# First LayerNorm of a transformer block: statistics finished in four groups of four token tiles instead of one group of sixteen

## What is computed

```python
x = x + 0.5 * ffn(layernorm(x))        # routed "spline" FFN, 64 experts in 8 clusters, then a LayerNorm
x = x + attn(layernorm(x))             # causal, 16 query heads on 4 kv heads, LayerNorm, output projection
x = x + 0.5 * ffn(layernorm(x))        # the same FFN again

def layernorm(x, eps=1e-5):
    m = mean(x, axis=-1); v = var(x, axis=-1)
    return (x - m) / sqrt(v + eps)
```

## Time and profile before

| | us |
|---|---|
| median of 2 runs | 1165.7 (1164.79 to 1166.62) |
| the profiled execution | 1164.39 |
| span of its slowest core (core 1), first to last instruction | 1162.9 |
| spans of the 8 cores | 1151.6 to 1162.9 |
| busy on core 1: PE, ACT, DVE | 802.9, 511.3, 479.7 |

### The profile page before, as it was taken

How to read it: one execution, slowest core, us unless ns; L and a number is a source line. 1 busy time by engine, 2 the same in 40 slices (tenths; PEclk the granted TensorE clock), 3 DMA queues, 4 the chain that set the end, 5 groups by cost and what they waited for, 6 DMA issues and landing times.

```text
span 1162.9 us, 12643 instructions; the slowest of 8 cores (1151.6 to 1162.9 us)
## 1 busy us (share of the span) xinstructions
PE 802.9 (69%) x3804; PEld 322.3 (28%) x3804; DVE 479.7 (41%) x912; ACT 511.3 (44%) x497; POOL 13.7 (1%) x21
## 2 busy tenths in 40 slices
PE   3087561796999457587788788886069968766197
PEld 1053210334444113222222222222034325311032
DVE  1853815685000554533522241113225564580643
ACT  1061331006223455378888988997171006233100
POOL 0100000000000000000000000000000010000000
PEclk9988855555999566589999989998558996865555
DMA  6800000008000000000000000000500012000024
GB/s 153 187 2 0 1 0 0 1 1 109 1 1 1 1 0 1 1 1 1 1 1 1 1 1 1 1 1 1 73 1 1 1 12 21 1 1 0 0 117 173
DMA packets 23872, 25.24 MB, mean 22 GB/s; under 512 B 13178, under 2 KB 17531, under 8 KB 23810
## 3 DMA queue, kind: packets, MB, share of 16 engines
q0 software_dynamic: 12208, 7.09, 5.1%
q1 hardware_dynamic: 11602, 17.34, 4.6%
HBM read 23.13 MB, written 8.39 MB: 27 GB/s over the span
## 4 chain that ended last, share of the span: by engine, by line
PE 50%; ACT 19%; DVE 14%; issue 8%; DMA 6%; SPq 1%; DVEq 1%; ACTq 0%; POOL 0%; POOLq 0%
ACT sE L1395 11%; PE pQ L938 7%; PE pW L1324 5%; PE pO L1139 5%; PE pTR L361 5%; PE pS L1197 4%; PE pH L624 3%; ACT sHH L1395 3%; PE pD L855 3%; PE pD L844 3%; PE pD L849 3%; DMA sX<-x 3%; PE pM L698 3%; PE pS L677 2%; DMA sWV<-wv 2%
## 5 line engine op out<-in xcount | busy, mean ns | idle before, releaser
L1395 ACT ACTIVATE sE<-pS,sNB 128x1024 bf16<-128x1024 f32 (+1 forms) x320 | 296.8, 990 | 71.4 <-PE pS L1197 69.5
L1139 PE MATMUL pO<-sE,sVTM 128*65 128x512 bf16 (+3 forms) x640 | 194.6, 389 | 23.5 <-DVE sTMPA L1395 23.1
L1197 PE MATMUL pS<-sQT,sKT 64*128 64x512 bf16 (+3 forms) x640 | 124.7, 381 | 59.9 <-DVE sE L1395 32.9
L361 PE MATMUL pTR<-sIDB,sXFB 128*128 128x128 bf16 x512 | 73.5, 262 | 66.1 <-ACT sXFB L1395 65.8
L1395 DVE TENSOR_TENSOR sE<-sE,sTRI 128x256 bf16<-128x256 bf16 x128 | 37.1, 291 | 162.0 <-ACT sE L1395 161.3
L1197 PEld LDWEIGHTS pS<-sQT,sKT 64*128 64x128 bf16 x640 | 36.6, 94 | 178.9 <-issue 176.8
L361 PEld LDWEIGHTS pTR<-sIDB,sXFB 128*128 128x128 bf16 x512 | 53.0, 104 | 88.7 <-issue 70.2
L1395 ACT ACTIVATE sRS<-sSCR 128x16 f32<-128x16 f32 x6 | 1.4, 229 | 168.5 <-DVE sSCR L1395 168.5
L1139 PEld LDWEIGHTS pO<-sE,sVTM 128*65 128x65 bf16 x640 | 47.5, 115 | 96.0 <-issue 90.7
L1395 DVE BATCH_NORM_STATS2 sSTAT<-sX 128x6 f32<-128x512 f32 x96 | 60.3, 686 | 11.3 <-ACT sGB L1395 6.1
L1324 PE MATMUL pW<-sWO,sT 128*128 128x512 bf16 x256 | 62.4, 388 | 0.0
(11 more groups left out here) (176 smaller groups left out, 835.1 us busy)
## 6 DMA issues: line engine op xcount, KB each, us to landing
sX<-x SPq DMA_DIRECT2D x4, 2048.0 KB, 20.0
y<-sX SPq DMA_DIRECT2D x16, 512.0 KB, 2.6
sWQ<-wq POOLq DMA_DIRECT2D x1, 2048.0 KB, 17.5
sWO<-wo POOLq DMA_DIRECT2D x1, 2048.0 KB, 16.6
sW1C<-cw POOLq DMA_DIRECT2D x2, 512.0 KB, 11.1
sWK<-wk POOLq DMA_DIRECT2D x1, 512.0 KB, 22.0
sWV<-wv POOLq DMA_DIRECT2D x1, 512.0 KB, 24.5
sSGR<-sigsT SPq DMA_DIRECT2D x1, 256.0 KB, 19.0
```

The costliest lines, as they stand in the source:

```text
L361: tt.transpose(pTR[:, par, c, :], sXFB[:, par, 128 * c:128 * (c + 1)], sIDB[:]),
L1139: mi = t.matmul(pO[:, h, lv:512], sVTM[:, c, gg, :], sE[:, epar, h, lv:512], start=(c == 0), stop=(c == cmax - 1))
L1197: mi = t.matmul(pS[:, cpar, h, lv:512], sKT[o:o + 64, kchunk, 128 * c:128 * (c + 1)], sQT[o:o + 64, hp, q0:qe], start=True, stop=True, til ...
L1395: self._last = a(*args, **kw)
```

## The change

`emit_ln_stats` gets a branch `quarters`, used by the first LayerNorm alone. It takes the tiles in four groups: 8 `bn_stats`, then their 8 `bn_aggr`. The tail of a group (9 operations, the square root, 6 operations, now on 128 x 4 operands) is emitted behind the `bn_aggr` of the next group. `emit_ln_transpose` gets `aux_tiles`: the normalisation of tile t waits for the tail of its own group, not for one mark of all tiles. The number of `bn_stats` and `bn_aggr`, the arithmetic on each element, the transposes and the copies stay the same.

```diff
+    def emit_ln_stats(src_tiles, rs_out, tile_waits=None, quarters=False):
+        if quarters:
+            auxq = [None] * 4
+            agq = []
+            for q in range(4):
+                for t in range(4 * q, 4 * q + 4):
+                    ap = src_tiles(t)
+                    tw = tile_waits[t] if tile_waits else []
+                    P.st("v", lambda v, t=t, ap=ap:
+                         v.bn_stats(sSTAT[:, t, 0:6], ap[:, 0:512]), wait=tw)
+                    P.st("v", lambda v, t=t, ap=ap:
+                         v.bn_stats(sSTAT[:, t, 6:12], ap[:, 512:1024]))
+                sm = P.mark("v", "AUX")
+                for i, t in enumerate(range(4 * q, 4 * q + 4)):
+                    P.st("v", lambda v, t=t: v.bn_aggr(sMV4[:, t, 0:2], sSTAT[:, t, 0:6]),
+                         wait=[sm] if i == 0 else [])
+                    P.st("v", lambda v, t=t: v.bn_aggr(sMV4[:, t, 2:4], sSTAT[:, t, 6:12]))
+                agq.append(P.mark("v", "AUX"))
+                if q >= 1:
+                    auxq[q - 1] = emit_ln_stats_tail(rs_out, [agq[q - 1]],
+                                                     (4 * (q - 1), 4 * q))
+            auxq[3] = emit_ln_stats_tail(rs_out, [agq[3]], (12, 16))
+            return auxq
...
-    def emit_ln_stats_tail(rs_out, wait0):
+    def emit_ln_stats_tail(rs_out, wait0, ts=(0, NT)):
+        t0, t1 = ts
+        sMV4s = sMV4[:, t0:t1]
+        sSCRs = sSCR[:, t0:t1]
+        rs_out = rs_out[:, t0:t1]
...
-            w = list(aux_ready) if isinstance(aux_ready, list) else [aux_ready]
+            if aux_tiles is not None:
+                w = [aux_tiles[t]]
+            else:
+                w = list(aux_ready) if isinstance(aux_ready, list) else [aux_ready]
...
+        elif first:
+            tw = [[xld[t // 4]] for t in range(NT)]
+            aux = emit_ln_stats(lambda t: sX[:, t, :], sRS, tile_waits=tw, quarters=True)
...
-        lnv = emit_ln_transpose(lnes, lambda t: sX[:, t, :], sRS, aux)
+        if isinstance(aux, list):
+            lnv = emit_ln_transpose(lnes, lambda t: sX[:, t, :], sRS, None,
+                                    aux_tiles=[aux[t // 4] for t in range(NT)])
```

More of the change, by code:

```diff
@@ L287, in build_program @@
     setup_es.close()
-    def emit_ln_stats(src_tiles, rs_out, tile_waits=None):
+    def emit_ln_stats(src_tiles, rs_out, tile_waits=None, quarters=False):
[21 more added lines that the diff above has]
+            return auxq
         for t in range(NT):
@@ L301, in emit_ln_stats @@
         return emit_ln_stats_tail(rs_out, [ag_mark])
-    def emit_ln_stats_tail(rs_out, wait0):
[L304 to L310, removed]
+    def emit_ln_stats_tail(rs_out, wait0, ts=(0, NT)):
[3 more added lines that the diff above has]
+        rs_out = rs_out[:, t0:t1]
+        m1 = sMV4s[:, :, 0:1].rearrange("p t o -> p (t o)")
+        v1 = sMV4s[:, :, 1:2].rearrange("p t o -> p (t o)")
+        m2 = sMV4s[:, :, 2:3].rearrange("p t o -> p (t o)")
+        v2 = sMV4s[:, :, 3:4].rearrange("p t o -> p (t o)")
+        mu = sSCRs[:, :, 2:3].rearrange("p t o -> p (t o)")
+        sc0 = sSCRs[:, :, 0:1].rearrange("p t o -> p (t o)")
+        sc1 = sSCRs[:, :, 1:2].rearrange("p t o -> p (t o)")
         rs = rs_out[:, :, 0:1].rearrange("p t o -> p (t o)")
@@ L337, in emit_ln_stats_tail, with emit_ln_transpose @@
         return P.mark("v", "AUX")
-    def emit_ln_transpose(stack, src_tiles, rs, aux_ready, src3d=False):
+    def emit_ln_transpose(stack, src_tiles, rs, aux_ready, src3d=False, aux_tiles=None):
         pTR = psum(stack, "pTR", [128, 3, NC, 128], BF16)
@@ L425, in emit_ffn @@
             aux = emit_ln_stats_tail(sRS, [pre_ag])
-        else:
-            tw = [[xld[t // 4]] for t in range(NT)] if first else None
-            aux = emit_ln_stats(lambda t: sX[:, t, :], sRS, tile_waits=tw)
+        elif first:
+            tw = [[xld[t // 4]] for t in range(NT)]
+            aux = emit_ln_stats(lambda t: sX[:, t, :], sRS, tile_waits=tw, quarters=True)
+        else:
+            aux = emit_ln_stats(lambda t: sX[:, t, :], sRS)
         if first:
@@ L449, in emit_ffn @@
         lnes = ExitStack()
-        lnv = emit_ln_transpose(lnes, lambda t: sX[:, t, :], sRS, aux)
+        if isinstance(aux, list):
+            lnv = emit_ln_transpose(lnes, lambda t: sX[:, t, :], sRS, None,
+                                    aux_tiles=[aux[t // 4] for t in range(NT)])
+        else:
+            lnv = emit_ln_transpose(lnes, lambda t: sX[:, t, :], sRS, aux)
         ses = ExitStack()
```

## The result

The changed kernel takes 1175.41 us (median of 12 runs) against 1165.33 us (median of 10) for the kernel before on the same chips; the ratio is 1.008, with a 95% interval of 1.0061 to 1.0099. The change makes it slower, by about 10 us. A few executions are 1 to 2.5% slower, at a lower granted clock on half of the cores and whatever the kernel; the ratios leave those out, the medians don't.

A forecast was written before the change was run, and what follows sets the result against it. The chain of waits in the first 80 us, with DVE full there, was taken to bound it. Core 1: 12.9 - 0.25 + 0.6 - 2.0 - 1.8 + 0.9 = +10.4 us, span 1173.3, forecast 1176 (1170 to 1181).

The forecast's parts named there:

- one more tail on DVE: First LayerNorm, DVE's list: each extra tail on 4 columns costs 4.3 us, three of them +12.9 us.
- the turn from `bn_stats` to `bn_aggr`: DVE, each group: switching from `bn_stats` to `bn_aggr` costs 0.19 us, three more turns +0.6 us (0 to 0.9).
- the last `stats_math`, narrower: DVE, fourth group's tail: `stats_math` on 4 columns is narrower by 9 steps, -0.25 us.
- wait for x: DVE's 1.99 us wait on core 1 for the last quarter of x goes, since DVE comes to it later.
- D: Distance from DVE's first `bn_stats` to `dsum`; predicted shift +12.4 us without a wait for x, +10.4 on core 1.
- ACT from its square root to tile 0: ACT's tile 0 needs only the first group's mark, so it needn't wait for the last `newton`: -1.8 us.
- late first copy, kept to `dsum`: `newton` and `tern` stand between ACT's start and DVE's first copy; PE can't catch up: +0.9 us (0 to 1.2).
- The order on ACT: ACT's list: tile 0 is queued behind the fourth group's square root, which takes the early start away.
- The first rival: First LayerNorm: the stage overlaps after all and DVE's own work binds, +4.7 us or 1170.4; chance 3%.
- low bound of 4.2: DVE tail on 4 columns: 4.2 us if each operation is as cheap as the narrowest row; 4.3 was taken.
- the estimate from it: DVE: by the skill's formula of (N + 151) cycles at 0.96 GHz, 45 more operations cost 7.2 us.
- a change of level in the expert loop: Rival, first FFN: PE's bursts run at 2.4 GHz after the shift, giving back 13.9 us, time 1162; chance 3%.

The follow-up runs named there:

- one-tail kernel: The change's four groups of `bn_stats` and `bn_aggr`, but a single tail on 16 columns behind them; 1166.9 us, ratio 0.9994.
- early-ACT kernel: The change with ACT's list reordered: tiles 0 to 3 behind the first square root, 4 and 5 behind the second; 1176.1 us, ratio 1.0094.
- four groups interleaved: The change with each group's normalisations, transposes and copies behind that group's tail on every engine, `tern` behind the last tail; 1173.4 us, ratio 1.0076.
- two-group kernel: The change with two groups of eight tiles instead of four of four, not interleaved; 1166.3 us, ratio 1.0000.
- short tail: Kernel before, ungrouped, one `bn_aggr` per tile and fewer `stats_math` and `newton` operations in three LayerNorms; 1160.8 us (0.9957), again 1158.1 (0.9930).
- the padding: Short tail plus twelve dependent 16-column DVE operations, result unread, behind the first LayerNorm's tail; 1157.3 us, ratio 0.9916.

## Why the prediction was right, step by step

The forecast was 1176 with a range of 1170 to 1181; the median is 1175.4. Its steps, with what the profile of the changed kernel and the experiments show:

| step | predicted us | measured us | read from |
|---|---|---|---|
| one more tail on DVE | 4.3 | 4.21 | 43.02 to 47.23 |
| the turn from `bn_stats` to `bn_aggr`, each | 0.19 | 0.20 | one-tail kernel, 0.61 / 3 |
| the last `stats_math`, narrower | -0.25 | -0.23 | 69.36 - 66.90 against 55.15 - 52.46 |
| wait for x | gone | gone | D alike on 8 cores |
| ACT from its square root to tile 0 | -1.8 | -1.9 | 69.48 - 69.36 = 0.12 against 57.20 - 55.15 = 2.05 |
| late first copy, kept to `dsum` | +0.9 | +0.96 | 90.95 - 69.48 = 21.47 against 77.71 - 57.20 = 20.51 |
| D, cores without a wait for x | +12.4 | +12.2 | 58.94 - 46.75 |
| D, core 1 | +10.4 | +10.1 | 58.94 - 48.84 |

**The order on ACT** was read rightly as keeping tile 0 behind the fourth square root. But the prediction also says that this order takes the early start away, and as a cause that is only half of it. The early-ACT kernel gave ACT its early start, 22 us sooner, and D stayed at 58.93: what holds the stage is DVE's list, on which the copies stand behind all four tails.

**The first rival** (full overlap, +4.7) describes the four groups interleaved. D came within 0.7 us of its bound, and the kernel was still slower than before.

**The tail's price.** The choice near the low bound of 4.2 was right. The Trainium skill (VectorE: DVE Perf Modes, The TRN2 errata) would put an operation on 4 columns at 161 ns, and the rows show 0.17. As a price of the tail the estimate from it is too little, since operations that wait for each other start 0.27 apart: 45 of them and three square roots took 12.6 us, not 7.2. The page's advice against many small operations holds, and more strongly than by its figure.

**The clock.** The prediction said that one core could move by 4 us against another, and it priced a change of level in the expert loop at 13.9 us. That loop stayed slow in all 12 profiles: behind its first pS its bursts took 1.88 to 1.89 us on every core. What did change its level lay just ahead of it, in pH, pC and the first pS. For single cores the 4 us were too little: behind `dsum`, core 0 became 7.7 us shorter and core 2 5.4 us longer than in the profile before, and core 1, for which the sum was made, grew by 6.9 us in all, not by 10.4. The mean over the cores hid this: the unedited stretches took 0.8 + 0.7 - 1.8 us against before, nearly nothing in sum. So part of the accuracy is luck: the two-group kernel, with a D forecast as well as this one, missed its time by 2 us, and the short tail missed the upper end of its range by 3. The slowest core also wasn't core 1, as summed, but core 5, with cores 3 and 7 within 2 us of it.

**What stays open.** Attention takes between 665 and 683 us over all cores and kernels, with the same code, and its mean over the cores between 671.4 and 676.9 from kernel to kernel. The shorter ones tend to have the higher granted clock (in the changed kernel 0.85 over the 667.5 us of core 0 and 0.83 over the 679.9 us of core 7), but I didn't find what sets it. Nor is it known why the padding changed the level in FFN 2. No run took the waits out of the tail. The padding bears on it: its twelve operations read nothing that the one before wrote but wait for it all the same, and they start 3.27 / 12 = 0.27 us apart like the others (56.03 to 59.30, core 1). So the price comes without a use of the result; whether it would go with the wait wasn't tried.

## What to carry to other kernels

Before splitting a late step so that its consumer can start early, write out each engine's list in the order of emission: here the consumer's first job (ACT's first tile) and DVE's copies, which the transposes need, both still stood behind the last piece. A chain of operations that wait for each other on 2 to 16 columns costs by its number of steps and hardly by its width, so shorten the chain first; splitting it multiplies it. And judge a change of a few microseconds by the distance between two landmarks around the edited stage: where no core waited for a DMA inside it, D was the same on all cores to 0.05 us, while their spans differed by 13 (1160.6 to 1173.5).

## What the runs showed of the hardware

- DVE operations that wait for the one before start 0.27 to 0.28 us apart on 2 to 8 columns (0.24 behind the first of a tail) and 0.27 to 0.29 on 16, while each is busy for 0.13 to 0.19 (a reciprocal up to 0.26). `bn_aggr`, without a wait between them, start 2.22 / 32 = 0.07 apart.
- `bn_aggr` over 12 values takes little more than over 6: 1.29 / 16 = 0.081 us against 2.22 / 32 = 0.069.
- The same 32 matmuls after the same 3.49 us of idle ran in 7.07 or 8.75 us, and in no other time in 12 profiles. In FFN 2 the slow case stood on 7 of 8 cores in both profiles of one kernel, and on none once twelve small operations had been put in 900 us ahead; the cause isn't known.
- The Trainium skill (TensorE: Matmul & The Clock Gate, Part 1) says that the number of slow matmuls at a kernel's start differs between runs of the same kernel. No run here counts those at the start. In the middle the traces show such a difference too: in FFN 1 of the short-tail kernel the second pH pass was slow on one core in the first profile and on four in the second.
